# Two reorderings and a new weight layout in a fused linear-attention and expert kernel on one Trainium2 core

## The chip, the cores and the metric

The kernel runs on one core of a Trainium2 chip. The metric is device time in microseconds. The engines are named as the profile names them: PE (TensorE, matmuls), PEld (its weight loads), DVE (VectorE), ACT (ScalarE), POOL (GpSimd) and SP (SyncE, which here only issues DMAs).

## The reference, cut to what matters

```python
xn = _layernorm(x)                                   # x: 1024 tokens x 256
x + attention(xn) + moe(xn)

# moe: 8 experts, one per token, and a shared expert
logits = xn @ router_w.T ; top_val, top_id = top_k(logits, 1)
xs = xn * sigmoid(top_val)
# expert e, for its own tokens:   w_gate_up[e]: 256 x 1024,  w_down[e]: 512 x 256
h = silu(xs @ gate[e]) * (xs @ up[e])                # 512 hidden units
o = h @ w_down[e]
# shared: the same with one set of weights, for all tokens
# attention: decayed running sums of k and k*v per head, out = q*kv / sum(q*k), times w_out
```

The hidden units of an expert are only summed over, so they may be dealt out to blocks in any order, as long as the columns of gate and up and the rows of down are dealt alike.

## The kernel before, in words

The order of work is written out by hand: each engine has its own program, and semaphores (named `s_...`) join them. The kernel has three stretches. In the first, up to about 50 us, PE makes q, k, v and the router's logits and then the shared expert's hidden layer (`shared_tile`), while DVE and ACT prepare them. DVE works out for every token a row in a DRAM buffer `sorted_rows` in which the tokens stand sorted by expert, in tiles of 144 slots. The buffer is first cleared by one large DMA (line 348); then POOL scatters the 1,024 scaled tokens into it with eight indirect DMAs (line 471), each after the zeros have landed.

In the second stretch PE works through the expert tiles; with these inputs there are eight, one for each expert. I number them 0 to 7. A tile goes like this:

- "Way in": SP fetches the tile's 160 rows with four DMAs of 40 KB (`sorted_load`, line 364) into `xg`, and DVE transposes them into `xgT` (`sorted_in`, line 823). There is one `xg` and one `xgT`. So the transpose for tile t+1 waits for all gate/up matmuls of tile t (`s_gup`), and the fetch for tile t+2 waits for that transpose (`s_xgc`).
- PE makes gate and up in three parts of 2, 1 and 1 blocks of 128 hidden units (line 1141, 32 matmul instructions per tile), ACT takes the silu of each part (line 605), DVE multiplies it with up (`expert_part`, line 851) into `hr`, and PE makes the down product in the same three parts (line 1150, 8 + 4 + 4 instructions).
- The result leaves PSUM by a DVE transpose (`rows_out`, line 846), and POOL stores it with four DMAs (line 324). PE may start the next down product only after that transpose.

DVE executes strictly in the order of its program. In `expert_tile` it stood: part 0, part 1, wait for the rows of the next tile, transpose them, part 2.

The weights of an expert are 1 MB of gate/up and 512 KB of down. There are three buffers for them; the third is `xT_raw` with `ez`, which earlier stages still use. SP is one queue: experts 0 and 1 are loaded early, then SP waits for the scatters, fetches the rows of tile 0, loads expert 2, fetches the rows of tile 1, and from then on alternates between the rows of tile t+2 and the refill of the buffer that tile t has freed (`refill`, lines 379 and 381).

In the third stretch, from about 99.5 us, PE makes the last shared tile, the shared down product and the attention's output product; POOL gathers the expert rows, and DVE adds everything up.

Of the kernel before, what the change touches and what calls it, by code (L numbers as in the profile page):

```python
# [13 lines left out]
P = 128  # L14
# [4 lines left out]
SLOTS = 144  # L19
# [6 lines left out]

def build(nc, x, w_qkv, w_out, decay_param, router_w, w_gate_up, w_down, shared_gate_up, shared_down, out):
    _, T, D = x.shape
    E, _, F2 = w_gate_up.shape
    F = F2 // 2  # L30
    NT = T // P
    KC = D // P
    FC = F // P
    NH = T // 512
# [14 lines left out]
    with ExitStack() as ctx:  # L49
        def sb(name, shape, dt):  # L50
            return ctx.enter_context(nc.sbuf_tensor(name, shape, dt))

        def sem(name):
            return ctx.enter_context(nc.semaphore(name))
# [91 lines left out]
        xgT = sb("xgT", [P, KC, NSQ * SQ], F32)  # L146
# [4 lines left out]
        gu_of = [gu[0][:, :, :], gu[1][:, :, :], xT_raw[:, :, :]]  # L151
# [65 lines left out]
        s_lrow = sem("s_lrow")  # L217
# [27 lines left out]
        s_q = sem("s_q")  # L245
# [45 lines left out]
        block = ctx.enter_context(nc.Block())  # L291

        gu_dram = w_gate_up.rearrange("e (p c) n -> e p c n", c=KC)
        dn_dram = w_down.rearrange("e (c p) n -> e p c n", p=P)


        LAST = NH * FC - 1
# [19 lines left out]
        def silu_part(h):  # L317
            row, col = SILU_AT[h]
            return act_sb[:, row, col:col + len(PARTS[h]) * SLOTS]
# [7 lines left out]
        def _(sp):  # L327
# [24 lines left out]
            def expert_load(e):  # L352
                sp.dma_start(gu_of[e][:, :, :], gu_dram[e]).then_inc(s_gu[e], 16)
                sp.dma_start(dn_of[e][:, :, :], dn_dram[e]).then_inc(s_dn[e], 16)
# [6 lines left out]
            def sorted_load(first, s_load):  # L361
                for q in range(P // SQ):
                    rows = sorted_rows[bass.ds(first, NSQ * SQ), q * SQ * KC:(q + 1) * SQ * KC]
                    sp.dma_start(xg[q * SQ:(q + 1) * SQ, :, :], rows.rearrange("(j p) f -> p j f", p=SQ)).then_inc(s_load, 16)  # L364
# [8 lines left out]
            def refill(e):  # L373
# [6 lines left out]
                sp.wait_ge(s_down, done)  # L380
                sp.dma_start(dn_of[p][:, :, :], dn_dram[e + 3]).then_inc(s_dn[p], 16)

            sp.wait_ge(s_scatter, 16 * NT)
            sp.wait_ge(s_wlk, 1)
            sp.wait_ge(s_wlv, 1)
            sp.wait_ge(s_wlq, 1)
            sorted_load(SLOTS, s_xg0)
            sp.wait_ge(s_lrow, 1)
            sp.wait_ge(s_q, 2 * NH)
            expert_load(2)  # L390

            sp.wait_ge(s_plan, 1)
            sp.wait_ge(s_xgc, 1)
# [244 lines left out]
        def _(dve):  # L638
# [122 lines left out]
            def half(a):  # L761
                return a % 2, slice(a // 2 * 512, (a // 2 + 1) * 512)
# [14 lines left out]
            for a in range(2 * NH):  # L777
                c, cols = half(a)
# [43 lines left out]
            def sorted_in():  # L822
                V.transpose(xgT[:, :, :], xg.rearrange("p j (f c) -> p c j f", c=KC)).then_inc(s_xgc, 1)  # L823
# [24 lines left out]
            def expert_part(t, h):  # L848
                f, width = PARTS[h][0], len(PARTS[h])
                dve.wait_ge(s_silu, 3 * t + (h + 1))  # L850
                V.tensor_tensor(hr[:, f:f + width, :].rearrange("p f s -> p (f s)"), silu_part(h),  # L851
                                ps[:, UP[h], 0:width * SLOTS], ALU.mult).then_inc(s_hr, 1)

            def expert_tile(t):
                expert_part(t, 0)
                expert_part(t, 1)
                dve.wait_ge(s_xg, 64 * t + 64)
                dve.wait_ge(s_gup, 3 * t + 3)
                sorted_in()
                expert_part(t, 2)  # L860

            def head_reciprocals(part):
                cols = slice(part * P, (part + 1) * P)
# [14 lines left out]
            def first_tile(t):  # L878
                if t >= 3:
                    dve.wait_ge(s_ystore[(t - 1) % 2], 64 * ((t - 1) // 2))  # L880
                if t:
                    rows_out(t, (t - 1) % 2, s_yrow)
                expert_tile(t)
# [35 lines left out]
            with dve.Fori(E - 1, total) as t:  # L919
                dve.wait_ge(s_yfree, t - (E - 2))  # L920
                rows_out(t, 2, s_yrow)
                expert_tile(t)
# [26 lines left out]
        def _(pe):  # L949
# [178 lines left out]
            for e in range(E):  # L1128
                p = e % 3
                pe.wait_ge(s_gu[p], 16 * (e // 3) + 16)  # L1130
                with pe.Fori(ends[e - 1] if e else 0, ends[e]) as t:
                    pe.wait_ge(s_xgc, t + 1)
                    for h in range(3):
                        if e == 0 and h == 2:
                            pe.wait_ge(s_denc, 1)
                            pe.wait_ge(s_sh, LAST)
                        for u in range(2):
                            for j, f in enumerate(PARTS[h]):
                                for kc in range(KC):
                                    col = u * F + f * P  # L1140
                                    ins = mm(ps[:, (GATE, UP)[u][h], j * SLOTS:(j + 1) * SLOTS],  # L1141
                                             gu_of[p][:, kc, col:col + P], xgT[:, kc, 0:SLOTS], start=(kc == 0), stop=(kc == KC - 1))
                        ins.then_inc(s_gup, 1)
                    pe.wait_ge(s_yrow, t + 1)
                    pe.wait_ge(s_dn[p], 16 * (e // 3) + 16)
                    for h in range(3):
                        pe.wait_ge(s_hr, 3 * t + (h + 1))
                        for c in range(KC):
                            for f in PARTS[h]:
                                ins = mm(ps[:, 5 + c, 0:SLOTS], dn_of[p][:, f, :].rearrange("p (m c) -> p c m", c=KC)[:, c, :], hr[:, f, :],  # L1150
                                         start=(f == 0), stop=(f == FC - 1))
                    ins.then_inc(s_down, 1)
# [62 lines left out]
```

## Time and profile before

| | |
|---|---|
| time, median of 3 runs | 124.27 us (124.21 to 124.7) |
| the profiled execution: its time | 124.46 us |
| the profiled execution: its span | 122.8 us |
| granted TensorE clock | 1.0 of full speed throughout |
| PE busy | 116.4 us (95%) |
| PEld busy | 100.6 us (82%) |
| DVE busy | 83.8 us (68%) |
| DMA | 25.18 MB in 21,069 packets |

The span runs from the first to the last instruction that the profiler shows; the time has 1.7 us more around it. Start times in the views are counted from the start of the span. A row of a timeline gives start, duration, engine, line, operation, what it writes and reads, how many instructions are merged in it, and in brackets how long the engine stood idle before it and what ended that.

### The profile page before, as it was taken

Reading aid. Unit: us, or ns where it says so; the run is one execution under the profiler, and the core shown is the slowest. Engines: PE = TensorE matmul, PEld = TensorE weight load, DVE = VectorE, ACT = ScalarE, POOL = GpSimd, SP = SyncE. Lnnn points to the kernel's source line nnn. Section 1 sums busy time; section 2 is a strip of 40 time slices with the busy share of each in tenths; the row PEclk is TensorE's granted clock in tenths of the full one; section 3 lists DMA queues with packets and bytes.
Section 4 is the critical chain, followed back from the end, with each engine's and each line's share of the span. In section 5 each row is a group of like instructions: output and inputs, shape, how many; then the busy total and the mean of one; then the engine's idle time right before and its main releaser. Section 6 shows DMA issues by size and latency. Waiting matters only on the chain.

```text
span 122.8 us, 2394 instructions
## 1 busy us (share of the span) xinstructions
PE 116.4 (95%) x757; PEld 100.6 (82%) x757; DVE 83.8 (68%) x186; ACT 47.2 (38%) x93; POOL 44.9 (37%) x80
## 2 busy tenths in 40 slices
PE   4989999999999999997999899999899999999991
PEld 1257876788888875997999899999799988999990
DVE  0789678999969996929692939696623456933382
ACT  0667799917987845420303030323030308100000
POOL 7904040018688800000617070704360600887300
PEclk9999999999999999999999999999999999999999
DMA  3692799999999525861799999999941322233254
GB/s 94 179 323 31 284 331 238 165 166 187 404 398 390 213 61 83 334 189 37 193 358 314 339 243 355 285 351 310 324 111 44 68 57 52 59 91 112 85 185 156
DMA packets 21069, 25.18 MB, mean 205 GB/s; under 512 B 9081, under 2 KB 18817, under 8 KB 20033
## 3 DMA queue, kind: packets, MB, share of 16 engines
q1 hardware_dynamic: 18128, 20.91, 58.9%
q0 software_dynamic: 1664, 3.25, 8.3%
q10 hardware_dynamic: 1264, 0.88, 2.3%
q8 instruction: 6, 0.10, 0.3%
q14 instruction: 7, 0.05, 0.1%
HBM read 18.95 MB, written 6.08 MB: 204 GB/s over the span
## 4 chain that ended last, share of the span: by engine, by line
PE 40%; DMA 38%; POOL 6%; SPq 6%; issue 4%; DVE 3%; POOLq 0%; ACTq 0%; DVEq 0%
DMA sorted_rows<-zeros 17%; PE ps L1141 16%; DMA wqkv<-sorted_rows 13%; PE ps L1150 7%; POOL sorted_rows L471 6%; PE ps L313 6%; PE ps L315 6%; PE ps L314 5%; SPq L364 4%; DMA wqkv<-in_L_attn_w_qkv_dram 4%; DMA x_sb<-in_L_attn_x_dram 2%; DVE xgT L823 2%; DMA sorted_rows<-xn,slot_row 2%; SPq L330 1%; DVE wqkv L851 1%
## 5 line engine op out<-in xcount | busy, mean ns | idle before, releaser
L324 POOL DMA_DIRECT2D sorted_rows<-yrow x28 | 16.1, 579 | 38.2 <-DVE yrow L846 37.9
L1141 PE MATMUL ps<-xgT,gu 128*128 128x144 f32 x192 | 24.5, 286 | 0.0
L1141 PEld LDWEIGHTS ps<-xgT,gu 128*128 128x128 f32 x192 | 24.0, 190 | 0.1
L605 ACT ACTIVATE rz<-ps 128x144 f32<-128x144 f32 (+1 forms) x24 | 7.9, 330 | 36.4 <-PE ps L1141 36.4
L851 DVE TENSOR_TENSOR wqkv<-rz,ps 128x144 f32<-128x144 f32 (+1 forms) x24 | 8.1, 340 | 8.9 <-ACT rz L605 8.8
L1150 PE MATMUL ps<-wqkv,dn 128*128 128x144 f32 x96 | 13.0, 288 | 0.7 <-DVE wqkv L851 0.7
L1150 PEld LDWEIGHTS ps<-wqkv,dn 128*128 128x128 f32 x96 | 12.3, 197 | 1.0 <-DVE wqkv L851 1.0
L313 PE MATMUL ps<-xT_hi,sgu_hi 128*128 128x512 f32 x32 | 12.9, 402 | 0.0
L315 PE MATMUL ps<-xT_hi,sgu_lo 128*128 128x512 f32 x32 | 12.7, 396 | 0.0
L314 PE MATMUL ps<-xT_lo,sgu_hi 128*128 128x512 f32 x32 | 12.7, 396 | 0.0
L494 POOL DMA_INDIRECT q_sb<-sorted_rows,done_row x8 | 8.4, 1048 | 8.8 <-DMA sorted_rows<-yrow 6.7
L471 POOL DMA_INDIRECT sorted_rows<-xn,slot_row x8 | 9.6, 1204 | 3.2 <-issue 2.1
L823 DVE STREAM_TRANSPOSE xgT<-wqkv 128x320 f32<-128x320 f32 x9 | 4.6, 512 | 7.9 <-DMA wqkv<-sorted_rows 6.7
L315 PE MATMUL ps<-wqkv_hi,hT_lo 128*128 128x256 f32 x32 | 9.1, 283 | 0.0
L313 PE MATMUL ps<-wqkv_hi,hT_hi 128*128 128x256 f32 x32 | 9.1, 283 | 0.0
L314 PE MATMUL ps<-wqkv_lo,hT_hi 128*128 128x256 f32 x32 | 9.0, 280 | 0.0
L1141 PE MATMUL ps<-xgT,xT_raw 128*128 128x144 f32 x64 | 8.2, 286 | 0.0
L313 PEld LDWEIGHTS ps<-xT_hi,sgu_hi 128*128 128x128 f32 x32 | 6.0, 188 | 2.4 <-issue 1.1
L1141 PEld LDWEIGHTS ps<-xgT,xT_raw 128*128 128x128 f32 x64 | 8.0, 190 | 0.0
L1025 PE MATMUL ps<-xT_lo,wqkv_hi 128*128 128x512 f32 x24 | 7.7, 403 | 0.0
L936 DVE TENSOR_TENSOR x_sb<-x_sb,q_sb 128x256 f32<-128x256 f32 x8 | 3.4, 433 | 6.0 <-DMA q_sb<-sorted_rows,done_row 6.0
L315 PEld LDWEIGHTS ps<-xT_hi,sgu_lo 128*128 128x128 f32 x32 | 6.0, 188 | 1.5
(166 smaller groups left out, 228.7 us busy)
## 6 DMA issues: line engine op xcount, KB each, us to landing
gu<-in_L_ffn_w_gate_up_dram SPq DMA_DIRECT2D x6, 1024.0 KB, 6.6
dn<-in_L_ffn_w_down_dram SPq DMA_DIRECT2D x6, 512.0 KB, 8.2
sorted_rows<-zeros SPq DMA_DIRECT2D x1, 2608.0 KB, 20.4
xT_raw<-in_L_ffn_w_gate_up_dram SPq DMA_DIRECT2D x2, 1024.0 KB, 5.2
wqkv<-sorted_rows SPq DMA_DIRECT2D x40, 40.0 KB, 2.9
sorted_rows<-yrow POOLq DMA_DIRECT2D x28, 40.0 KB, 5.1
sgu<-_ffn_shared_gate_up_dram SPq DMA_DIRECT2D x1, 1024.0 KB, 6.1
ez<-in_L_ffn_w_down_dram SPq DMA_DIRECT2D x2, 512.0 KB, 6.8
```

The lines of the kernel that those rows point to most:

```text
L313: nc.tensor.matmul(o, w_hi, m_hi, start=start, stop=False)
L314: nc.tensor.matmul(o, w_hi, m_lo, start=False, stop=False)
L315: return nc.tensor.matmul(o, w_lo, m_hi, start=False, stop=stop)
L324: eng.dma_start(rows.rearrange("(j p) f -> p j f", p=SQ), yrow[q * SQ:(q + 1) * SQ, b, :, :]).then_inc(s_store, 16)
L471: pool.indirect_dma_start(sorted_rows, bass.IndirectOffsetOnAxis(ap=slot_row[:, i:i + 1], axis=0), xn[:, i, :], None).then_inc(s_scatter, 16)
L494: pool.indirect_dma_start(y_tok[:, i, :], None, sorted_rows, bass.IndirectOffsetOnAxis(ap=done_row[:, i:i + 1], axis=0)).then_inc(s_gather ...
L605: A(silu_part(h), ps[:, GATE[h], 0:len(PARTS[h]) * SLOTS], ACT.Silu).then_inc(s_silu, 1)
L823: V.transpose(xgT[:, :, :], xg.rearrange("p j (f c) -> p c j f", c=KC)).then_inc(s_xgc, 1)
L851: V.tensor_tensor(hr[:, f:f + width, :].rearrange("p f s -> p (f s)"), silu_part(h), ps[:, UP[h], 0:width * SLOTS], ALU.mult).then_inc(s_h ...
L1025: ins = mm(o, wqkv_hi[:, kc, cols], xT_lo[:, kc, rows], start=False, stop=last and kc == KC - 1)
L1141: ins = mm(ps[:, (GATE, UP)[u][h], j * SLOTS:(j + 1) * SLOTS], gu_of[p][:, kc, col:col + P], xgT[:, kc, 0:SLOTS], start=(kc == 0), stop=(k ...
L1150: ins = mm(ps[:, 5 + c, 0:SLOTS], dn_of[p][:, f, :].rearrange("p (m c) -> p c m", c=KC)[:, c, :], hr[:, f, :], start=(f == 0), stop=(f == ...
```

## The change

Four edits, of which the last two belong together:

1. On SP the load of expert 2 moves ahead of the wait for the scatters, with the two waits that it needs itself (`s_lrow`, `s_q`).
2. On DVE `expert_part(t, 2)` moves ahead of the wait for the next tile's rows and of their transpose.
3. The rows of `w_down` are dealt to partitions as (p c) in place of (c p): partition p gets rows 4p to 4p+3, which lie together in DRAM, one run of 4 KB in place of four of 1 KB.
4. To match, block f of gate and of up is now every fourth column, starting at f, in place of 128 columns side by side. PE's weight load reads them with a step of 16 bytes.

```diff
-        dn_dram = w_down.rearrange("e (c p) n -> e p c n", p=P)
+        dn_dram = w_down.rearrange("e (p c) n -> e p c n", c=FC)
...
+            sp.wait_ge(s_lrow, 1)
+            sp.wait_ge(s_q, 2 * NH)
+            expert_load(2)
             sp.wait_ge(s_scatter, 16 * NT)
             sp.wait_ge(s_wlk, 1)
             sp.wait_ge(s_wlv, 1)
             sp.wait_ge(s_wlq, 1)
             sorted_load(SLOTS, s_xg0)
-            sp.wait_ge(s_lrow, 1)
-            sp.wait_ge(s_q, 2 * NH)
-            expert_load(2)
...
             def expert_tile(t):
                 expert_part(t, 0)
                 expert_part(t, 1)
+                expert_part(t, 2)
                 dve.wait_ge(s_xg, 64 * t + 64)
                 dve.wait_ge(s_gup, 3 * t + 3)
                 sorted_in()
-                expert_part(t, 2)
...
-                                    col = u * F + f * P
+                                    units = gu_of[p][:, kc, u * F:(u + 1) * F].rearrange("p (m f) -> p f m", f=FC)[:, f, :]
                                     ins = mm(ps[:, (GATE, UP)[u][h], j * SLOTS:(j + 1) * SLOTS],
-                                             gu_of[p][:, kc, col:col + P], xgT[:, kc, 0:SLOTS], start=(kc == 0), stop=(kc == KC - 1))
+                                             units, xgT[:, kc, 0:SLOTS], start=(kc == 0), stop=(kc == KC - 1))
```

On SP, at the place where the first expert loads give way to the fetch of sorted rows, the difference between the two programs is as follows. `xT_raw` and `ez` are the third expert's buffers; the first `wqkv<-sorted_rows` fetches the rows of tile 0, the next those of tile 1.

```order
 L351 DMA wout<-in_L_attn_w_out_dram 128x2x256
 L353 DMA gu<-in_L_ffn_w_gate_up_dram 128x2048
-L354 DMA dn<-in_L_ffn_w_down_dram 128x4x256
+L354 DMA dn<-in_L_ffn_w_down_dram 128x1024
 L353 DMA gu<-in_L_ffn_w_gate_up_dram 128x2048
-L354 DMA dn<-in_L_ffn_w_down_dram 128x4x256
-L364 DMA wqkv<-sorted_rows 32x5x64 x4
+L354 DMA dn<-in_L_ffn_w_down_dram 128x1024
 L353 DMA xT_raw<-in_L_ffn_w_gate_up_dram 128x2048
-L354 DMA ez<-in_L_ffn_w_down_dram 128x4x256
-L364 DMA wqkv<-sorted_rows 32x5x64 x4
+L354 DMA ez<-in_L_ffn_w_down_dram 128x1024
+L364 DMA wqkv<-sorted_rows 32x5x64 x8
```

The third expert's two loads now stand ahead of the fetch for tile 0, and the fetches for tiles 0 and 1 stand next to each other.

On DVE, at tile 0 (the row of L823 is the transpose of the rows for tile 1; the rows of L851 ahead of it are parts of tile 0, and L887, L802 and L846 are what follows the tile):

```order
 L813 TENSOR_TENSOR hT_lo<-sgu,hT_hi 128x512 x2
 L851 TENSOR_TENSOR wqkv<-rz,ps 128x288
-L851 TENSOR_TENSOR wqkv<-rz,ps 128x144
+L851 TENSOR_TENSOR wqkv<-rz,ps 128x144 x2
 L823 STREAM_TRANSPOSE xgT<-wqkv 128x320
-L851 TENSOR_TENSOR wqkv<-rz,ps 128x144
 L887 TENSOR_SCALAR sgu<-sgu 128x512
 L802 SCALAR_TENSOR_TENSOR kvsum<-decay,kvsum 128x512 x2
 L846 STREAM_TRANSPOSE yrow<-ps 128x2x160
```

The third product (128x144) has moved from behind the transpose to ahead of it; nothing else moved. The same happens in all eight tiles.

## Rows read from the trace of the kernel before

**Rows 1.** Timeline of PE through the eight expert tiles
```profile
49.82 4.08 PE L1141 MATMUL ps<-xgT,gu 128*128 128x144 f32 x32
...
56.12 0.77 PE L1150 MATMUL ps<-wqkv,dn 128*128 128x144 f32 x4 [0.75 <-DVE wqkv L851]
56.72 4.08 PE L1141 MATMUL ps<-xgT,gu 128*128 128x144 f32 x32
...
62.60 4.08 PE L1141 MATMUL ps<-xgT,xT_raw 128*128 128x144 f32 x32
...
69.08 4.08 PE L1141 MATMUL ps<-xgT,gu 128*128 128x144 f32 x32
...
80.84 4.08 PE L1141 MATMUL ps<-xgT,xT_raw 128*128 128x144 f32 x32
...
87.60 4.08 PE L1141 MATMUL ps<-xgT,gu 128*128 128x144 f32 x32
...
99.45 0.51 PE L1089 MATMUL ps<-att_lo,head_row 16*128 16x512 f32 x4
```

**Rows 2.** Timeline of DVE: transposes of sorted rows, and two products
```profile
48.84 0.51 DVE L823 STREAM_TRANSPOSE xgT<-wqkv 128x320 f32<-128x320 f32 x1 [0.67 <-DMA wqkv<-sorted_rows]
...
55.36 0.51 DVE L823 STREAM_TRANSPOSE xgT<-wqkv 128x320 f32<-128x320 f32 x1 [1.78 <-DMA wqkv<-sorted_rows]
...
60.91 0.51 DVE L823 STREAM_TRANSPOSE xgT<-wqkv 128x320 f32<-128x320 f32 x1 [0.43 <-PE ps L1141]
...
67.72 0.51 DVE L823 STREAM_TRANSPOSE xgT<-wqkv 128x320 f32<-128x320 f32 x1 [1.35 <-DMA wqkv<-sorted_rows]
...
79.15 0.51 DVE L823 STREAM_TRANSPOSE xgT<-wqkv 128x320 f32<-128x320 f32 x1 [0.42 <-PE ps L1141]
...
84.16 0.63 DVE L851 TENSOR_TENSOR wqkv<-rz,ps 128x288 f32<-128x288 f32 x2
86.24 0.51 DVE L823 STREAM_TRANSPOSE xgT<-wqkv 128x320 f32<-128x320 f32 x1 [1.44 <-DMA wqkv<-sorted_rows]
```

**Rows 3.** Timeline of ACT: the silu of tile 1's third part
```profile
60.84 0.29 ACT L605 ACTIVATE rz<-ps 128x144 f32<-128x144 f32 x1 [0.69 <-PE ps L1141]
```

**Rows 4.** Windows of the tile stretch: last two figures DMA share, GB/s
```profile
58.24:89.00 30.76, 29.84 (x241) 29.42 (x241) 21.60 (x44) 5.68 (x16) 11.81 (x21) 1.00 0.97 307
```

**Rows 5.** Timelines of DVE, POOL and SP: last q, last scatter, first fetch, third expert
```profile
33.15 0.67 DVE L789 SCALAR_TENSOR_TENSOR q_sb<-ps,ez 128x512 f32<-128x512 f32 x1
...
42.08 1.11 POOL L471 DMA_INDIRECT sorted_rows<-xn,slot_row  x1 [0.30 <-issue]
...
44.63 2.77 SPq L364 DMA_DIRECT2D wqkv<-sorted_rows  x4
47.50 0.38 SPq L353 DMA_DIRECT2D xT_raw<-in_L_ffn_w_gate_up_dram  x1
```

**Rows 6.** The scatter issued at 31.42: count, us from issue to landing
```profile
sorted_rows<-xn,slot_row POOLq DMA_INDIRECT x1, 7.0
```

**Rows 7.** The scatter of 42.08; and the fetch for tile 1 (from 49.43)
```profile
sorted_rows<-xn,slot_row POOLq DMA_INDIRECT x1, 2.5
...
wqkv<-sorted_rows SPq DMA_DIRECT2D x4, 40.0 KB, 4.8
```

**Rows 8.** Windows around the scatters and the third expert's load, columns as above
```profile
37.00:40.00 3.00, 3.00 (x15) 2.41 (x14) 3.00 (x4) 2.35 (x5) 2.41 (x2) 1.00 1.02 399
40.00:42.00 2.00, 2.00 (x10) 1.63 (x9) 1.87 (x4) 1.46 (x3) 1.47 (x2) 1.00 0.64 244
50.20:51.80 1.60, 1.60 (x16) 1.60 (x15) 1.51 (x3) 0.63 (x1) 0.00 (x0) 1.00 0.98 405
52.00:53.00 1.00, 1.00 (x10) 1.00 (x9) 0.60 (x2) 0.43 (x2) 0.00 (x0) 1.00 1.08 382
```

**Rows 9.** Lines, PEld: loads of neighbouring columns and of every second one
```profile
L1141 PEld LDWEIGHTS ps<-xgT,gu 128*128 128x128 f32 x192 | 24.0, 190 | 0.1
L1150 PEld LDWEIGHTS ps<-wqkv,dn 128*128 128x128 f32 x96 | 12.3, 197 | 1.0 <-DVE wqkv L851 1.0
```

## Prediction

> **What bounds the kernel now.** I read the profile in this order. The page's busy times, in the table above, say that PE is busy for 116.4 us of a span of 122.8 us at the full clock. So a gain has to come from PE's few gaps, or from fewer or faster matmuls, and this change removes none. Next the timeline of PE, for the gaps. In the second stretch the gate/up product of tile 1 starts at 56.72 and that of tile 2 at 62.60 [rows 1]: a tile that waits for nothing takes PE 5.88 us. Eight of them are 47.04 us. The stretch runs from 49.82 to 99.45, 49.63 us, with 0.1 us behind the last matmul. So 2.5 us are waits, and three tiles hold them: from 49.82 to 56.72 are 6.90 us (1.02 over), from 62.60 to 69.08 are 6.48 (0.60 over), from 80.84 to 87.60 are 6.76 (0.88 over) [rows 1]. That is all that edits 1 and 2 can win in this stretch.
>
> Then the timeline of DVE, for what these waits are. In each of the three the transpose of the next tile's rows started late and was released by the DMA that fetches them: at 55.36, 67.72 and 86.24 [rows 2]. The next gate/up product started 1.36 us after each (56.72, 69.08, 87.60). Of these, 0.51 us are the transpose, and the rest is the third product, which stands behind it on DVE, and then the last four down instructions, which PE held back for that product (the row of 56.12 names the product as what ended PE's wait) [rows 1, 2]. PE had work left, and the work was queued behind a transfer that it did not need.
>
> Last the view of windows: from 58.24 to 89.00 the DMA engines are busy for 0.97 of the time, at 307 GB/s [rows 4]. DMA is nearly a second bound here, and a late fetch is a fetch that stands behind a refill of weights.
>
> **Edit 2, the third product first.** Where rows are late, PE can finish the down product while they are on their way. From the transpose's start to gate/up then come its 0.51 us and a hop, for which I take 0.06: 0.57 in place of 1.36, 0.79 less. That covers the second wait (0.60), most of the first (0.24 left) and of the third (0.09 left). The price: where the rows are early, the transpose starts right behind gate/up now (60.91, released by PE) and will wait for the silu and the product. The silu starts at 60.84 and takes 0.29 [rows 3]; with the hops and the product's own slot of 0.2 that puts the transpose at about 61.46, 0.55 later. PE does not feel it in that tile, since it has a down product of 1.96 us to do. But SP issues the next fetch only after the transpose, so that fetch moves by 0.55 too. From 60.91 to 67.72 are 6.81 us, and from 79.15 to 86.24 are 7.09 [rows 2]. Counted from tile 1's gate/up (G = 56.72), the transpose was at G + 4.19 and would be at G + 4.74; the next but one would start gate/up at G + 4.74 + 6.81 + 0.57 = G + 12.12, where two undisturbed tiles give G + 11.76 and the trace has G + 12.36. So alone this edit wins 0.24 of the 0.60 there, and by the same sum (80.84 less 5.88 as G) 0.25 of the 0.88. Alone it is worth 0.24 + 0.25 + 0.79 = 1.3 us.
>
> One more thing is late next. In tile 4 DVE has a long list behind its transpose (79.15), and the products of tile 5's first two parts came out at 84.16 to 84.79 [rows 2], just as PE wanted them (80.84 + 3.92 = 84.76). With the transpose 0.55 later and a product of 0.2 moved ahead of it, they come 0.35 later and PE waits. I take 0.2 us for that.
>
> **Edit 1, the third expert early.** It needs DVE's last q, which starts at 33.15 and takes 0.67 [rows 5]. So SP issues the load at about 33.9 and not at 47.50. Two things follow.
>
> (a) The fetch for tile 1 no longer stands behind 1.5 MB: it landed 4.8 us after issue, the fetch for tile 0 had an empty queue and its first DMA, issued at 44.63, let the transpose start at 48.84 [rows 2, 5, 7]. The first wait (1.02) goes altogether. Every later refill keeps its distance to the transpose before it, while gate/up starts sooner after that transpose; the fetch for tile 3 then meets a refill that is 0.33 us further on (the two transposes lie 5.88 us apart in place of 5.55, 55.36 to 60.91), and 6.81 becomes about 6.5. With that the second wait goes too (G + 11.81 against 11.76).
>
> (b) The DMA queue ran dry at about 41: its share is 1.02 from 37 to 40 and 0.64 from 40 to 42 [rows 8]. Now 1.57 MB more follow. At 399 GB/s, shared with what is left of the scatters (0.5 MB), they run until about 46. The last three scatters were issued into a queue that was emptying: the one of 42.08 landed after 2.5 us, where the first, issued into a full queue, took 7.0 [rows 5 to 7]. SP can't fetch tile 0 before all have landed, and PE has only 0.4 us to spare there (transpose from 48.84 to 49.35, gate/up at 49.82). The delay lies between nothing (the scatters' share of the queue is served at once) and 4.5 us (7.0 less 2.5). The full end is unlikely, because the first scatter stood behind the loads of experts 0 and 1 and the last would stand behind one load that is partly done. I take 1.2 us, about a quarter of the way; less the 0.4, PE starts the tiles 0.8 us later, at 50.65.
>
> The rule that bears on this is in the Trainium skill, "DMA: Bandwidth & Descriptors", section "Queues, rings and completion order": each DMA engine takes turns between queues packet by packet. By that rule a scatter would wait for a packet or so, and edit 1 would cost next to nothing. The first scatter's 7.0 us [rows 6] do not look like taking turns, so I give the rule a rival's place and not the sum.
>
> **Edit 3, runs of 4 KB.** From 50.20 to 51.80, with gate/up of the third expert in runs of 8 KB, the queue moved 405 GB/s; from 52.00 to 53.00, with mostly its down weights in runs of 1 KB, 382 [rows 8]. For 0.52 MB that is 1.37 us against 1.29: 0.08 us for each load. It shortens each fetch that stands behind a refill by as much. I count nothing for it on its own; in four refills it takes 0.3 us out of the nearly full queue, and leaves about 0.3 of the third wait in place of 0.6 (0.88 less 0.25). The bounds are nothing and 0.3.
>
> **Edit 4, every fourth column.** There are 256 such weight loads (8 tiles of 32), each of them ahead of a matmul instruction, and PE takes one pair each 5.88 / 48 = 0.1225 us. No row shows a step of 16 bytes. The nearest is the down product, whose weights are read with a step of 8 bytes: 197 ns from start to end against 190 for neighbouring columns [rows 9], at the same pace (the 16 down instructions take the 1.96 us of 5.88 that 16 pairs should). I take nothing: if each doubling of the step adds 7 ns to a load that lies beside the matmul before it, it stays hidden. From below, a gain is excluded, as a wider step can't make a load shorter than what is hidden now. From above: if a load could no longer overlap at all, a pair would take 204 ns in place of 122.5, and 256 pairs 21 us more.
>
> Here a rule speaks against the change: the Trainium skill, "Advanced Engine Details and Errata", section "SBUF Cachelines", says that a line of SBUF is 16 bytes and that at least two accesses have to fall on one line to hide its latency. The down product's step just meets that (two a line) and its row agrees; the new step has one a line. By that rule the sum would end well above 124, by the row it does not change.
>
> **Sum**, against the profiled execution (124.46 us, span 122.8 and 1.7 around it): waits removed 2.5; left of the third wait 0.3; DVE's list in tile 5 0.2; later start 0.8. Net 2.5 - 0.3 - 0.2 - 0.8 = 1.2 us less, 123.26. The third stretch only shifts: PE is busy in it to the end. The median of the runs shown is 0.2 lower (124.27), so I predict 123.1.
>
> **The rivals.**
> 1. The early load costs nothing (the scatters take turns). For it: from 37 to 40 scatters and weights ran together at 399 GB/s and POOL's issues were spaced as before. Against it: 7.0 us. Then 123.1 - 0.8 = 122.3, and with nothing left of the third wait 122.0.
> 2. The scatters stand behind the whole third load. With a delay of 2.9 to 4.5 us the tiles start 2.5 to 4.1 us later, where the sum has 0.8: 123.1 + 1.7 to 3.3 gives 124.8 to 126.4. It ends slower from a delay of the last scatter of about 3 us (2.4 for no change).
> 3. The step of 16 bytes costs pace. A pair has to lose only 5 ns for 256 x 5 = 1.3 us, which undoes the gain; 20 ns make 5.1 us, 128.2; the bound is 144.
> 4. Little changes: the DMA engines at 0.97 give the waits back tile by tile, as each refill plus fetch takes longer than 5.88 us. From the transpose at 55.36 to that at 86.24 there are five tiles in 30.88 us, 6.18 each, against 5.88 on PE. If that is the queue's own pace, 0.9 us stay in place of 0.3, and with the later start it is 123.7 to 124.3.
>
> **How the numbers follow.** Likeliest, the sum above with a delay of the scatters of 0.6 to 2: 0.42, range 122.4 to 123.9. Rival 1: 0.14. Rival 4: 0.14. Rival 2: 0.12. Rival 3: 0.18, of which 0.05 lie within 1.3 us. 0.5% (0.6 us) is what a measurement of this kernel can tell from no change: under 123.65 is faster, over 124.9 slower. Faster: 0.38 of the first, 0.14 of rival 1, 0.03 of rival 4, 0.01 of others: 0.56. Slower: 0.10 of rival 2, 0.15 of rival 3: 0.25. The same: 0.19. The range from 121.8 to 125.6 leaves out most of rival 3 and half of rival 2.
>
> **What would show it.** In the timeline of PE after the change: eight starts of gate/up 5.88 us apart, but for one or two tiles with 0.2 to 0.3 more; the first at about 50.6. On SP, the third load issued at 33.9, and the first fetch at about 45.9. On DVE, transposes behind PE's waits at gate/up + 4.74. In the lines, the weight load of line 1141 at 197 to 211 ns and the pace of 0.1225 us kept. The prediction is wrong if that pace is not kept, or if the first fetch is issued past 47.

## The result, and the profile after

The changed kernel takes 151.51 us (median of 4 runs, 150.98 to 151.68) where the kernel before takes 124.26 (124.21 to 124.7): a ratio of 1.2255, with an interval of 1.2163 to 1.2348. It is 27 us slower. 123.1 was predicted, in a range of 121.8 to 125.6. Every ratio in this document compares only executions that lie within 1.5% of the fastest of their own kernel, with a 95% interval.

The page's line on the engines, for the span of 149.9 us:

```profile
PE 144.3 (96%) x757; PEld 128.8 (86%) x757; DVE 84.0 (56%) x186; ACT 47.2 (31%) x93; POOL 44.6 (30%) x80
PEclk9999999999999999999999999999999999999999
```

PE executes the same 757 matmuls as before, at the same full clock, and is busy for 27.9 us more; PEld for 28.2 us more. DVE, ACT and POOL are within 0.3 us of where they were. So time was not lost in waiting: some of PE's instructions became longer. The timeline of PE through the first tiles and at the end of the last one says which:

```profile
50.91 7.75 PE L1141 MATMUL ps<-xgT,gu 128*128 128x144 f32 x32 [0.82 <-DVE xgT L823]
58.49 2.12 PE L1150 MATMUL ps<-wqkv,dn 128*128 128x144 f32 x16
60.45 7.63 PE L1141 MATMUL ps<-xgT,gu 128*128 128x144 f32 x32
67.91 2.12 PE L1150 MATMUL ps<-wqkv,dn 128*128 128x144 f32 x16
69.87 7.63 PE L1141 MATMUL ps<-xgT,xT_raw 128*128 128x144 f32 x32
...
126.51 0.51 PE L1089 MATMUL ps<-att_lo,head_row 16*128 16x512 f32 x4
```

These answer to [rows 1]. A down product starts 7.46 us after its gate/up product (60.45 to 67.91), where the profile before has about 3.92; the down product still takes 1.96 (58.49 to 60.45). No brackets follow after the first row: PE never waits between tiles. The pace of a pair of weight load and matmul in gate/up is 7.46 / 32 = 0.233 us in place of 0.1225. The groups of weight loads, which answer to [rows 9] (busy time, mean ns of one):

```profile
L1141 PEld LDWEIGHTS ps<-xgT,gu 128*128 128x128 f32 x192 | 45.3, 329 | 1.3 <-DVE xgT L823 1.3
L1150 PEld LDWEIGHTS ps<-wqkv,dn 128*128 128x128 f32 x96 | 12.3, 198 | 0.0
```

A gate/up load takes 329 ns from start to end in place of 190. The down product's loads, which PE reads with the same step as before, stay at 198 (197 before).

The other steps can be read in the queues. On SP, where third load and first fetch stand (they answer to [rows 5]), and the transposes on DVE:

```profile
33.99 0.33 SPq L353 DMA_DIRECT2D xT_raw<-in_L_ffn_w_gate_up_dram  x1
...
46.97 14.81 SPq L364 DMA_DIRECT2D wqkv<-sorted_rows  x12
```

```profile
50.34 0.51 DVE L823 STREAM_TRANSPOSE xgT<-wqkv 128x320 f32<-128x320 f32 x1 [2.07 <-DMA wqkv<-sorted_rows]
...
59.01 0.31 DVE L851 TENSOR_TENSOR wqkv<-rz,ps 128x144 f32<-128x144 f32 x1 [1.56 <-ACT rz L605]
59.23 0.51 DVE L823 STREAM_TRANSPOSE xgT<-wqkv 128x320 f32<-128x320 f32 x1
```

The third load is issued at 33.99, as forecast (33.9). The first fetch is issued at 46.97 (forecast 45.9), and the first transpose at 50.34 is released by it, 3.37 us after the issue. The second transpose follows the third product at once; the rows were there.

The difference adds up. Gate/up: 256 pairs x (0.2331 - 0.1225) = 28.3 us more. Start of the tiles: 50.91 less 49.82 = 1.1 more. From there to the end of the last tile, 75.60 us are 8 x 9.42 and 0.24 of rest, where before 49.63 were 8 x 5.88 and 2.59: 2.35 less. The rest of the program: 23.39 against 23.35. In all 27.1, and the spans differ by 27.1 (149.9 less 122.8).

### The profile page after: what moved, and what is told of

It is laid out like the page before. It is cut to its first block, busy times and chain, and to the rows that moved or that the text cites. A ratio compares the mean times of both kernels' runs of the same rounds, so it can differ in the third digit from the quotient of the medians.

```text
span 149.9 us, 2395 instructions
## 1 busy us (share of the span) xinstructions
PE 144.3 (96%) x757; PEld 128.8 (86%) x757; DVE 84.0 (56%) x186; ACT 47.2 (31%) x93; POOL 44.6 (30%) x80
## 4 chain that ended last, share of the span: by engine, by line
PE 64%; DMA 23%; POOL 5%; issue 2%; SPq 2%; DVE 1%; POOLq 0%; ACTq 0%
PE ps L1141 40%; DMA sorted_rows<-zeros 14%; PE ps L1150 10%; POOL sorted_rows L471 5%; PE ps L313 5%; PE ps L315 4%; PE ps L314 4%; DMA sorted_rows<-xn,slot_row 3%; DMA wqkv<-in_L_attn_w_qkv_dram 3%; DMA x_sb<-in_L_attn_x_dram 2%; DMA wqkv<-sorted_rows 1%; SPq L364 1%; SPq L330 1%; DVE xgT L823 0%; POOLq L475 0%
## 5 line engine op out<-in xcount | busy, mean ns | idle before, releaser
L1141 PE MATMUL ps<-xgT,gu 128*128 128x144 f32 x192 | 45.9, 397 | 0.8 <-DVE xgT L823 0.8
L1141 PEld LDWEIGHTS ps<-xgT,gu 128*128 128x128 f32 x192 | 45.3, 329 | 1.3 <-DVE xgT L823 1.3
L851 DVE TENSOR_TENSOR wqkv<-rz,ps 128x144 f32<-128x144 f32 (+1 forms) x24 | 8.5, 354 | 41.6 <-ACT rz L605 41.6
L1141 PE MATMUL ps<-xgT,xT_raw 128*128 128x144 f32 x64 | 15.3, 397 | 0.0
L1141 PEld LDWEIGHTS ps<-xgT,xT_raw 128*128 128x128 f32 x64 | 15.1, 329 | 0.0
L314 PEld LDWEIGHTS ps<-xT_lo,sgu_hi 128*128 128x128 f32 x32 | 6.0, 188 | 1.4
L577 ACT ACTIVATE hT_hi<-sgu 128x512 fp32r<-128x512 f32 x8 | 5.1, 632 | 6.5 <-DVE sgu L820 6.5
```

The lines of the kernel that those rows point to most:

```text
L314: nc.tensor.matmul(o, w_hi, m_lo, start=False, stop=False)
L577: A(hT_hi[k // FC][:, k % FC, :], h_sb[:, k % 2, :], ACT.Copy).then_inc(s_shh, 1)
```

## The experiments

The theory: the whole loss lies in the weight loads with a step of 16 bytes, and it is paid per 16-byte line that a load visits, 1.82 ns each. Rivals: the loads suffer from DMA traffic that the new orders or the 4 KB runs bring; or the cost grows with the distance in bytes; or load and matmul have stopped overlapping, so that their times add (0.11 for the load and 0.12 for the matmul would also make 0.233). A second question came up on the way: why the reorderings bring nothing once the layout is taken back.

### The two halves of the change

Edits 1 and 2 with the old layout:

```diff
-        dn_dram = w_down.rearrange("e (p c) n -> e p c n", c=FC)
+        dn_dram = w_down.rearrange("e (c p) n -> e p c n", p=P)
...
-                                    units = gu_of[p][:, kc, u * F:(u + 1) * F].rearrange("p (m f) -> p f m", f=FC)[:, f, :]
+                                    col = u * F + f * P
...
-                                             units, xgT[:, kc, 0:SLOTS], start=(kc == 0), stop=(kc == KC - 1))
+                                             gu_of[p][:, kc, col:col + P], xgT[:, kc, 0:SLOTS], start=(kc == 0), stop=(kc == KC - 1))
```

> Edits 1 and 2 alone, the old weight layout. Theory (the weight loads with a step of 16 bytes carry the whole loss: 256 pairs at 0.233 us in place of 0.1225, 28.4 us; the reorderings do what the changed kernel's timeline shows: no waits between tiles, first gate/up at 50.9): pairs back at 0.1225 us, starts of gate/up 5.88 to 6.2 us apart, time 122.9 to 123.6 us. Rival (the early load and the full DMA queue slow PE's weight loads too, by SBUF traffic): pairs stay above 0.13 us and the time above 126.

Measured: 0.9985 of before (0.993 to 1.004). Pairs are back at 0.1225 us (60.32 to 64.24 for 32), but for about fourteen of tile 0, over which the granted clock was at its lower level. The rival falls. The first gate/up started only at 52.67 in this profile; the last section shows that tile.

Edits 3 and 4 with the old orders:

> Edits 3 and 4 alone, the old orders. Theory: pairs of gate/up at 0.233 us, 28.4 us more than before; the three waits of before vanish too, since a tile of 9.4 us outlasts every fetch (less 2.5 us, but the third product still stands behind a transpose), so 149.5 to 150.8 us. Rival (the loss needs the new orders): under 145 us.

Measured: 150.34 us, 1.2184 of before (1.2111 to 1.2256). The pairs take 0.233 us, and gate/up starts 9.43 us apart (9.31 from tile 0 to tile 1). The layout alone makes the loss. With tiles that long no fetch is late, also with the old order on DVE; the transpose now waits for PE instead, 1.31 us each time:

```profile
57.74 0.51 DVE L823 STREAM_TRANSPOSE xgT<-wqkv 128x320 f32<-128x320 f32 x1 [1.31 <-PE ps L1141]
58.17 0.27 DVE L851 TENSOR_TENSOR wqkv<-rz,ps 128x144 f32<-128x144 f32 x1
```

### What a weight load costs at other steps

All runs here have edits 1 and 2. Step of 3 columns (12 bytes), then of 8 (32 bytes), both with the old down layout:

```diff
-    gu_of[p][:, kc, u * F:(u + 1) * F].rearrange("p (m f) -> p f m", f=FC)[:, f, :]
+    gu_of[p][:, kc, u * F + f:u * F + f + 3 * P - 2:3]                                # step of 3
+    gu_of[p][:, kc, :].rearrange("p (m s) -> p s m", s=8)[:, u * FC + f, :]           # step of 8
```

> Edits 1 and 2, the old layout of the down weights, gate/up blocks of 128 columns taken with a step of 3 (12 bytes); the blocks then don't match the down weights, so the values differ from the reference. Theory (a load pays 233/128 = 1.82 ns for each 16-byte line that it goes to next, which a step of 4 meets 128 times, a step of 3 96 times, a step of 2 64 times): a pair takes 0.175 us, 256 pairs 13 us more than hidden ones, about 137 us. Rival (a load is slowed only when no two neighbouring elements share a line): 0.1225 us, about 124 us. Second rival (any step that is not a power of two is as slow as 4): 0.233 us.

> As the run before with a step of 8 columns (32 bytes) over the whole gate/up row; values differ from the reference. Theory (lines): still one line for each element, so 0.233 us a pair as with a step of 4, about 151.5 us. Rival (the cost grows with the distance in bytes): from 0.1225 at 8 bytes and 0.233 at 16 bytes on, over 0.4 us a pair, over 190 us.

Measured, in one execution each: 135.65 us for a step of 3 and 151.7 for 8, beside 122.58 of before on the same chip. PE's timelines, of the step of 3 and then of the step of 8:

```profile
57.45 5.76 PE L1141 MATMUL ps<-xgT,gu 128*128 128x144 f32 x32
63.05 2.12 PE L1150 MATMUL ps<-wqkv,dn 128*128 128x144 f32 x16
```

```profile
59.48 7.78 PE L1141 MATMUL ps<-xgT,gu 128*128 128x144 f32 x32
67.10 2.12 PE L1150 MATMUL ps<-wqkv,dn 128*128 128x144 f32 x16
```

5.60 us / 32 = 0.175 us a pair, which is what 96 lines of 1.82 ns make; 256 pairs are 13.4 us more, and the time is 13.1 above before. At a step of 8 it is 7.62 / 32 = 0.238, 2% over the step of 4, though the elements lie twice as far apart. The rivals of this pair of runs fall: all or nothing (0.1225), as slow as a step of 4 (0.233), and cost by distance (over 0.4).

Then the load by itself. If a matmul moves 72 columns in place of 144, it is done sooner, and a pair shows the load's own time:

```diff
-    ins = mm(ps[:, (GATE, UP)[u][h], j * SLOTS:(j + 1) * SLOTS],
+    ins = mm(ps[:, (GATE, UP)[u][h], j * SLOTS:j * SLOTS + SLOTS // 2],
...
-    xgT[:, kc, 0:SLOTS], start=(kc == 0), stop=(kc == KC - 1))
+    xgT[:, kc, 0:SLOTS // 2], start=(kc == 0), stop=(kc == KC - 1))
...
-    hr[:, f, :],                  # moving operand of the down product, into ps[:, 5 + c, 0:SLOTS]
+    hr[:, f, 0:SLOTS // 2],       # into ps[:, 5 + c, 0:SLOTS // 2]
```

> Edits 1 and 2, old layout; gate/up and down products move 72 of the 144 slots only, so half of the tokens' expert results are left out. With half the columns a matmul instruction needs only about 0.06 us, and the pace of pairs shows the weight load's own time, where it is longer. Theory (lines): gate/up with neighbouring columns 0.105 to 0.110 us or below, the down product with its step of 8 bytes 0.116 us (64 lines of 1.82 ns). Rival (the load with a step of 2 costs no more than one of neighbours): the same pace for both.

> The changed kernel with 72 of 144 slots moved in both products (half of the tokens' expert results are left out). Theory (the weight load alone sets the pace at a step of 16 bytes): gate/up pairs stay at 0.233 us although the matmul has half the work. Rival (load and matmul no longer overlap, and their times add: 0.11 + 0.12): 0.17 us.

The timeline of the run with neighbouring columns, and a window of it (the third figure from the right is the granted clock):

```profile
55.50 3.74 PE L1141 MATMUL ps<-xgT,gu 128*128 128x72 f32 x32
59.07 2.05 PE L1150 MATMUL ps<-wqkv,dn 128*128 128x72 f32 x16
60.96 3.74 PE L1141 MATMUL ps<-xgT,xT_raw 128*128 128x72 f32 x32
...
50.00:60.00 10.00, 10.00 (x90) 10.00 (x89) 8.02 (x16) 2.62 (x8) 1.75 (x3) 1.00 0.32 81
```

3.57 / 32 = 0.112 us with neighbours and 1.89 / 16 = 0.118 with a step of 8 bytes in the down product, at the full clock. Halving the matmul hardly shortens the pair. So it isn't the matmul that sets this pace; I read 0.112 and 0.118 us as the loads' own time, just under the 0.1225 us that a pair with 144 columns takes. That is how little room the change had. What sets the 0.112 of neighbouring columns, the load itself or another floor of a pair, no run tells apart. The theory's 0.105 to 0.110 for neighbours was a little low, its 0.116 for 64 lines a little low too.

The run with a step of 16 bytes:

```profile
61.52 7.65 PE L1141 MATMUL ps<-xgT,gu 128*128 128x72 f32 x32
68.97 3.41 PE L1150 MATMUL ps<-wqkv,dn 128*128 128x72 f32 x15
...
60.00:70.00 10.00, 10.00 (x46) 10.00 (x46) 3.72 (x7) 0.99 (x3) 2.42 (x4) 0.50 0.56 190
```

Gate/up pairs stay at 7.45 / 32 = 0.233 us although the matmul has half the work. But in this window the granted clock is 0.50, the level of 1.2 GHz, at which pairs with 144 columns lie 0.240 us apart (the third profile of the kernel before, below). By that I estimate about 0.12 us for half the columns here, as much as all of them at the full clock, and the window can't tell the load alone from added times. The first pairs of tile 0 can, for the clock was still 1.00:

```profile
50.58:52.68 2.10, 2.10 (x9) 2.10 (x10) 1.87 (x4) 0.63 (x1) 0.00 (x0) 1.00 0.21 47
```

Nine matmuls start in these 2.10 us, 0.233 us for each. Added times (0.11 for the load and 0.06 for half a matmul, the rival's 0.17) would have let at least twelve start. So the load sets the pace alone, and that rival falls. At the clock of 0.50 it takes 0.233 us all the same, while the down product's loads, with 8 bytes, go from 0.118 to 0.213 us (61.52 less 58.11, by 16). The times of the two runs (133.07 and 164.44 us) can't be set beside others, because the clock fell in both.

Last, half of the step in a working kernel: pairs of blocks take every second column of 256, and the down weights come in runs of 2 KB to match.

```diff
+        dn_dram = w_down.rearrange("e (g p c) n -> e p g c n", g=2, c=2)
...
+    gu_of[p][:, kc, u * F + f // 2 * 2 * P:u * F + (f // 2 + 1) * 2 * P].rearrange("p (m c) -> p c m", c=2)[:, f % 2, :]
```

> Edits 1 and 2, and in place of the changed layout one with half of its step: block pairs of gate/up take every second column of 256 (8 bytes), the down weights come in runs of 2 KB to match. Theory (64 lines of 1.82 ns are 0.1165 us, under the 0.1225 us that the matmul needs): pairs at 0.1225 us, time as with edits 1 and 2 alone, 0.99 to 1.00 of before. Rival (a step of 2 costs in gate/up what it hides in the down product): over 1.01.

Measured: 1.010 (1.003 to 1.017), which is what the rival said. But its profile shows the pace of the theory:

```profile
55.70 4.08 PE L1141 MATMUL ps<-xgT,gu 128*128 128x144 f32 x32
59.62 2.12 PE L1150 MATMUL ps<-wqkv,dn 128*128 128x144 f32 x16
...
L1141 PEld LDWEIGHTS ps<-xgT,gu 128*128 128x128 f32 x192 | 24.0, 196 | 0.4 <-DVE xgT L823 0.2
```

3.92 / 32 = 0.1225 us, with loads of 196 ns. A step of 8 bytes costs gate/up nothing. The profiled execution took 122.78 us, the six runs lie between that and 124.79; with the third expert's load in another place the same layout measures 0.9993 (below). So the 1% does not come from the step. It rests on few executions, and what makes it stays open: the early load alone is no explanation, since the run with 4 KB runs has it too and measures 1.0006 (below), and edits 1 and 2 alone measure 0.9985.

| step (bytes) | lines visited | load, ns start to end | pair, us |
|---|---|---|---|
| 4 | 32 | 190 | 0.1225 (0.112 with 72 columns) |
| 8 | 64 | 196 | 0.1225 (0.118 with 72 columns) |
| 12 | 96 | 262 | 0.175 |
| 16 | 128 | 329 | 0.233 (0.233 with 72 columns, at either clock) |
| 32 | 128 | 335 | 0.238 |

### The edits one by one, and where their gain went

The third product first, alone:

> Edit 2 alone. Theory, by the sum of the prediction: 1.3 us less than before (0.24 + 0.25 + 0.79), less 0.2 for DVE's list in tile 5: about 123.2. Rival (what the earlier down product wins is lost again because every fetch is issued 0.55 us later): 124.0 to 124.6.

Measured: 1.0045 (0.9998 to 1.0092); neither gain nor clear loss. That is not the theory's 0.991 (123.2 by 124.27); the rival's range, 0.998 to 1.003, lies partly within the interval. What the edit does can be seen all the same. The tiles run from 49.89 to 97.93, with 0.9 us of waits in all. The first four gate/up products start 5.88 us apart, and at tile 5 stands the new wait that the prediction named, on the products that stand behind DVE's long list of tile 4:

```profile
79.39 4.11 PE L1141 MATMUL ps<-xgT,xT_raw 128*128 128x144 f32 x32
84.01 2.23 PE L1150 MATMUL ps<-wqkv,ez 128*128 128x144 f32 x16 [0.52 <-DVE wqkv L851]
86.08 4.08 PE L1141 MATMUL ps<-xgT,gu 128*128 128x144 f32 x32
```

The early load, alone:

> Edit 1 alone. Theory: the tiles start about 1.1 us later, as in the changed kernel (50.9 in place of 49.8), the wait of 1.02 us for tile 1 goes, the waits for tiles 3 and 6 stay: 124.0 to 124.6, no change. Rival (the first scatter's delay does not repeat without the 4 KB runs, the start stays at 49.9): 123.2.

Measured: 1.0058 (1.0002 to 1.0114). The first fetch was issued at 46.56 and gate/up started at 51.26, later as the theory said. There is no wait of 1.02 us for tile 1 (51.26 to 57.24), but none either in two of the three profiles of before, so this run doesn't show that the edit removed it. Of the two waits that should have stayed, the one for tile 3 is gone as well, and the one for tile 6 is there (80.77 to 87.39, 0.74 over).

The runs of 4 KB, with edits 1 and 2 and gate/up blocks of neighbouring columns:

```diff
-        dn_dram = w_down.rearrange("e (c p) n -> e p c n", p=P)
+        dn_dram = w_down.rearrange("e (p c) n -> e p c n", c=FC)
```

> Edits 1, 2 and 3, gate/up blocks of neighbouring columns as before; the down weights' rows then don't match them, so the values differ from the reference. Theory (the runs of 4 KB are worth 0 to 0.3 us, by 0.08 us a load): 0.99 to 1.00 of before, as edits 1 and 2 alone. Rival (shorter refills remove a wait that is left): 0.985 or less.

Measured: 1.0006 (0.996 to 1.0051). Longer runs bring nothing that this measurement can tell.

The third expert's load behind the fetch for tile 1, with edit 2:

```diff
-            sp.wait_ge(s_lrow, 1)
-            sp.wait_ge(s_q, 2 * NH)
-            expert_load(2)
             sp.wait_ge(s_plan, 1)
             sp.wait_ge(s_xgc, 1)
             sorted_load(2 * SLOTS, s_xg)
+            sp.wait_ge(s_lrow, 1)
+            sp.wait_ge(s_q, 2 * NH)
+            expert_load(2)
```

> Edit 2 alone of the change, and the third expert's load put behind the fetch for tile 1 in place of ahead of the scatters. Theory (the early load's gain came from getting out of the way of the fetch for tile 1, its loss from delaying the scatters; behind that fetch it has the gain without the loss): first gate/up at about 49.8, no waits over 0.3 us between tiles 0 and 2, 0.985 to 0.992 of before. Rival (the load now stands ahead of the fetch for tile 2, which becomes late instead): a wait at tile 2 of over 0.5 us and 0.995 or more.

> The run before with blocks of every second column and down weights in runs of 2 KB. Theory: the same time as the run before within 0.3%, or less by up to 0.2% for shorter down loads. Rival (a step of 2 in all loads costs): over 0.5% more than the run before.

Measured: 0.9996 (0.9961 to 1.0031) and 0.9993 (0.9949 to 1.0037). The profile is what the theory described (starts at 49.86, 55.74 and 61.62, the last tile ends at 97.58: 0.6 us of waits in all), but the ratio is not. So the question was not what these orders do, but what before does. Two more profiles of the kernel before, and one more of edits 1 and 2:

> The kernel before, unchanged, profiled once more. Theory (the fetches' landings differ from execution to execution, and the first profile of before happened to hold more waits than most): gate/up starts fit fewer waits than 2.5 us. Rival (2.5 us of waits are there every time): 2.3 us or more again, and the gain of the reorderings is lost elsewhere.

> The same again: between them the two tell how far the waits of before scatter. Theory: the sum of waits differs by 0.5 us or more between the profiles of before. Rival: within 0.3 us.

> Edits 1 and 2 with the old layout, profiled again. Theory: no wait over 0.3 us between tiles, one for DVE's list at tile 5, first gate/up at 50.5 to 52.7 by how late the last scatter lands. Rival (the start of 52.7 of the first profile was an exception of a disturbed run): 49.9.

PE's timeline in the second profile of the kernel before:

```profile
50.01 4.08 PE L1141 MATMUL ps<-xgT,gu 128*128 128x144 f32 x32
55.89 4.08 PE L1141 MATMUL ps<-xgT,gu 128*128 128x144 f32 x32
61.77 4.08 PE L1141 MATMUL ps<-xgT,xT_raw 128*128 128x144 f32 x32
68.01 4.08 PE L1141 MATMUL ps<-xgT,gu 128*128 128x144 f32 x32
...
98.00 0.51 PE L1089 MATMUL ps<-att_lo,head_row 16*128 16x512 f32 x4
```

From 50.01 to 98.00 are 47.99 us: 0.85 us of waits, by the sum that gave 2.5 for [rows 1]. The wait of 1.02 us for tile 1 isn't there: in this execution the scatters had landed earlier, the first fetch was issued at 43.40 (not 44.63) and the third load at 45.27 (not 47.50), and it was out of the way in time. The third profile is 4.2 us over the undisturbed pace (50.11 to 101.46) and took 126.45 us: 2.2 of them are a wait behind a single fetch, for which DVE stood idle for 2.92 us, and 1.7 are the tile after it, which ran at a lower clock (last section). So this sum differs by over 3 us from one execution of before to the next. Both expectations were met. What is left without it is nearly the same each time: 124.46 less 2.5, 123.02 less 0.85 and 126.45 less 4.2 are 122.0, 122.2 and 122.2 us. Edits 1 and 2, profiled again, hold 0.65 us of waits (50.04 to 97.83) and took 122.86 us. Their first gate/up at 50.04 misses the theory's 50.5 to 52.7 and lies near the rival's 49.9.

So where the second profile was taken, the waits that the reorderings take away are only some tenths of a microsecond larger than the ones that they leave; that is under what the comparisons can tell. The kernel before has a median of 122.86 us there. Where the change itself was measured it has 124.26, with its four times from 124.21 to 124.7, so there waits like those of the first profile (124.46) may have been the rule. Nor do the ratios say all: with every execution counted, the medians of the two runs with expert 2 behind the fetch are 122.84 and 122.78 beside 123.46 of before on the same chip, 0.5% less. Whether these orders shorten the longer executions stays open; the next run, on another chip, shows no such difference (123.14 beside 122.86).

The last run moves one of DVE's two long products from behind tile 4 to behind tile 5, on top of the run with expert 2 behind the fetch:

```diff
...
+            q_kv(0)
             first_tile(5)
+            q_kv(1)
```

> As the run with expert 2 behind the fetch for tile 1, and on DVE one of the two products of q and the kv sums (1.2 us) moved from behind tile 4 to behind tile 5. Theory (DVE's list delays tile 5's first products, and PE with them): the 6.1 us between the gate/up starts of tiles 5 and 6 go to 5.9, time 0.2 us less than that run, 0.99 to 0.998 of before. Rival (a late fetch holds tile 6 anyway): 6.1 us or more stay.

Measured: 1.0017 (0.9984 to 1.005). The stretch from tile 5 to 6 goes from 6.12 us to 6.00, near the 5.9 expected, and the waits in all from 0.6 to 0.2 us (49.98 to 97.34), but tiles 6 and 7 now take 5.98 each and the time shows nothing. No version here is shown to be faster than the kernel before.

## Why the prediction was wrong, point by point

**Edit 4 is the step that failed.** The prediction took nothing for "every fourth column", since each doubling of the step seemed to add 7 ns to a load that lies beside a matmul. Measured: 0.110 us for each of 256 pairs, 28.3 us. Two readings were wrong. Durations from start to end (190 and 197 ns) were taken for a small change on something well hidden. But loads overlap one another (each takes 190 ns, and one starts every 0.1225 us); the loads' own pace was 0.112 and 0.118 us, and the pace of the pairs could not show how close that was to 0.1225, because any value below looks the same. And the one known step, from neighbours to 8 bytes, was continued in a straight line. The measured steps fit a floor and a cost per line: 32 lines lie at the floor (0.112), 64 just above it, 96 and 128 at 1.82 ns each. The 1.82 is taken from the step of 16 bytes; the steps of 12 and 32 bytes (0.175 and 0.238 us) are what tests it. The bound from above, 21 us for loads that overlap nothing, was too low too, as it kept a duration of 204 ns; it was 329.

The rule of the Trainium skill that stood beside it ("Advanced Engine Details and Errata", section "SBUF Cachelines": at least two accesses on a 16-byte line) names the condition, and the step from 8 to 16 bytes agrees with it: hidden at two a line, 0.233 us at one a line. That a latency is what costs the time, no run shows. The step of 12 bytes, which the rule doesn't speak of, costs 0.175 us. The outcome stood among the rivals with a chance of 0.18; that third rival was right in kind (a pair loses pace) and beyond its own bound of 144 us in size.

**Edit 1**: (a) is not shown: the wait for tile 1 is gone wherever the load is early, but two of three profiles of before don't have it either. (b) The delay of the scatters was put at 1.2 us and the first fetch at 45.9; it was issued at 46.97 in the changed kernel, 2.3 us later than in the first profile of before. Over all profiles it was issued at 45.36 to 47.23 in the ten with the early load (mean 46.3) and at 43.08 to 44.63 in the eight without (mean 43.5): 2.7 us. About 0.5 us of this is that the last scatter was issued later on average. Counted from the issue of the last scatter, the first fetch follows after 2.40 to 2.55 us in the eight and after 3.4 to 5.3 in the ten. The size was low, the mechanism is shown. What PE sees of it varies: the tiles start at 49.8 to 52.7 in the ten and at 49.7 to 50.1 in the eight. The last scatter, which took 2.5 us to land [rows 7], took 4.8 in the changed kernel:

```profile
sorted_rows<-xn,slot_row POOLq DMA_INDIRECT x1, 4.8
```

The start of the tiles came near the forecast all the same (50.91, forecast 50.65) by an error the other way: the first transpose followed the fetch's issue after 3.4 us, where the first profile of before has 4.2 [rows 2, 5]. Rival 1, that the early load costs the scatters nothing, falls by the 4.8 us; how the queues share the engines, no run shows. The late start of rival 2 (2.5 us or more) stands in one of the ten profiles, with 52.67.

**Edit 2**: the sum gave 1.3 us alone; the run alone gave 1.0045. The steps are in its profile, with the price too: where the rows are early the transpose starts at gate/up + 4.67 (55.77 to 60.44), 0.48 later than before where 0.55 was forecast, and the wait at tile 5, taken at 0.2, is 0.52. What failed is the premise, "2.5 us are waits", as a sum that every execution has. It came from one execution, and in another it is 0.85.

**Edit 3**: counted was only 0.3 us, in the third wait (0.3 left in place of 0.6). The run with it measured 1.0006 and the one without 0.9985, on different chips, with intervals of half a percent: a gain of 0.3 us (0.24%) can be neither seen nor excluded.

**Rival 4**, that the DMA queue holds every tile to 6.18 us, falls: with edits 1 and 2 alone, five of the seven distances between gate/up starts are 5.88 us.

**The third stretch** shifts as a whole, 23.35 to 23.39 us, as forecast.

What stays open: why the time of single executions of these kernels scatters over 3 us (the fetches' landings differ, but what makes them differ no profile shows), and what costs the 1% of the run with a step of 2 and an early load.

## What to carry to other kernels

Before a weight block's access pattern is changed, count how many 16-byte lines a load of 128 columns will visit and compare 1.82 ns for each, as measured here for fp32, with the time of the matmul beside it; a step of two fp32 columns was free here and a step of four cost nine tenths of the pair again. A row that shows a pair's pace bounds the operation hidden in it from above only, so a hidden cost has to be measured by shortening what hides it. And where a gain is a sum of waits behind transfers, it should be read from more than one execution.

## What the runs showed of the hardware

Two things I had not expected. The load with a step of 16 bytes kept its 0.233 us when the granted clock fell from 1.00 to 0.50, while the load with a step of 8 bytes went from 0.118 to 0.213 us: the first is not paced by TensorE's clock. Neighbouring columns take 0.213 us at 0.50 too (96.20 to 103.03 for 32, in the run with half the columns), so at the lower clock a step of 8 bytes costs nothing even in the load's own time.

And PE's clock fell after PE had been kept waiting or had moved half the columns. In the first profile of edits 1 and 2, PE stood idle for 2.54 us ahead of the first tile, which then ran slower; the windows there (the clock is the third figure from the right):

```profile
48.00:52.00 4.00, 2.13 (x10) 1.37 (x8) 0.30 (x1) 1.12 (x2) 0.00 (x0) 1.00 0.20 45
52.00:54.00 2.00, 1.33 (x6) 1.34 (x7) 1.76 (x4) 0.00 (x0) 0.00 (x0) 0.69 0.09 20
54.00:58.00 4.00, 4.00 (x26) 4.00 (x26) 1.85 (x5) 1.33 (x3) 0.00 (x0) 0.73 0.14 31
58.00:62.00 4.00, 4.00 (x35) 4.00 (x34) 3.29 (x6) 0.29 (x1) 0.00 (x0) 1.00 0.11 25
```

The mean granted clock was 0.69 and 0.73 there, so partly at the lower level, and tile 0 took 7.65 us in place of 5.88. That execution took 126.84 us, 2.9 more than the median of its kernel. It shows what a late first fetch can cost beyond the wait itself: 1.8 us more in that tile. The third profile of the kernel before repeats it: PE was busy for 0.61 of 2.50 us, behind the late fetch, the clock fell, and the tile took 7.55 us.

```profile
79.50:82.00 2.50, 0.61 (x5) 0.55 (x5) 1.31 (x3) 0.00 (x0) 0.00 (x0) 1.00 1.03 355
82.00:84.00 2.00, 2.00 (x13) 2.00 (x13) 1.90 (x6) 0.72 (x1) 0.00 (x0) 0.69 0.40 108
84.00:86.00 2.00, 2.00 (x10) 2.00 (x10) 1.88 (x4) 0.41 (x1) 0.00 (x0) 0.50 0.37 58
```

With half the columns in the changed kernel it fell after an idle time of only 0.50 us: the clock was 1.00 from 50.58 to 52.68 and 0.56 in the 2.1 us after.
